# A gather-bound factorization machine: the quad that is kept raw moves from a block's eighth place to its sixth

## The chip, the core and the metric

The kernel runs on one core of one Trainium2 chip. The metric is device time in microseconds (us). The kernel before takes 735.56 us, the median of three runs (734.74 to 735.95).

## What is computed

For 2048 samples with 32 fields each, every field picks one row of 496 numbers out of its own table of 1250 rows, and the row is scaled with the sample's value of that field. Cut to what matters:

```python
gathered = table[f][xi[:, f]] for each field f      # (2048, 32, 496)
e  = gathered * xv[:, :, None]
s  = sum of e over the 32 fields
qi = 0.5 * (s * s - sum of e * e over the fields)    # (2048, 496)
h  = relu(xv @ W1 + b1)                              # (2048, 1024)
y  = concatenate([qi, h]) @ W2 + b2                  # (2048, 1)
```

All is float32. 2048 x 32 rows of 1984 bytes are 130 MB that have to be gathered from HBM.

## The kernel before

**Blocks and quads.** The batch is cut into 16 blocks of 128 samples, and the 32 fields of a block into eight quads. A quad is four fields of 128 samples: 512 rows in four groups of 128 partitions, each group fetched by one indirect DMA. So a block has eight quads (s = 0 to 7 in the code, "first" to "eighth" in the text) and 32 gathers, and the kernel has 128 quads and 512 gathers. Engines are named as in the profile: POOL (GpSimd), ACT (ScalarE), DVE (VectorE), PE (TensorE).

**Slots.** The rows land in the buffer `gathered`, which has eight slots. The quad with the running number n uses slot n % 8, so a block's quad s reuses the slot of the previous block's quad s. POOL issues the gathers in order (L218). Ahead of a quad's four gathers it waits until the slot's old quad is squared and has been summed (L210 to L214): for most quads the second is the semaphore `added`, raised by DVE, and for the quads of `block_quads` it is `summed`, raised by PE.

**Two ways through a block.** Seven of the quads are scaled in place (by ACT, L234, and the fifth by DVE, L447) and added up in PSUM by DVE (`running_ps`, L462); the last of these adds writes to `added_up` in SBUF. The one quad that is left, `block_quads = (7,)`, stays raw: ACT squares it with the value as a scale (L247), and PE sums it with the weights as the operand (L328, `sum_quad`). PE also sums `added_up` over the fields (L341, `sum_fields`), both into `sum_ps`. The last matmul of `sum_quad` raises `summed`. ACT then squares `sum_ps` (L254, `square_sums`), and that raises `sum_squared_ready`.

**Squares.** ACT squares the first quad from PSUM (L291), the second to fourth in one instruction of 5952 elements per partition (L241), and the fifth to seventh likewise. DVE weighs all squares with W2 (L435, eight instructions for a block).

**The hidden layer.** PE multiplies the block's values by W1 (L362, two instructions) and raises `hidden_ready`; DVE weighs the result with W2 (L528) and raises `hidden_used`.

**The order.** Each engine's instructions are written out in order, and every dependence between engines is a semaphore wait; there is no planner. PE's order in block i is: hidden layer of i (after `hidden_used` of i-1), wait for `sum_squared_ready` of i-1, wait for the last add of i, `sum_fields(i)`, `sum_quad(i * 8 + 7)`. ACT reaches `square_sums(i - 1)` behind the sixth quad of block i. The last block differs: its quads five to eight all stay raw.

**Entries.** In the trace each of PE's float32 matmuls stands as two weight loads (PEld) and two matmuls (PE). So the hidden layer of a block has 8 entries, `sum_fields` 16 and `sum_quad` 16, together 40.

Of the kernel before, what the change touches and what calls it, by code (L numbers as in the profile page):

```python
# [15 lines left out]
def fm_kernel(nc, index, value, value_t, emb, w1, b1, w2, b2, out):  # L16
# [23 lines left out]
    block_quads = (7,)  # L40
    wide = [0, 1, 2, 3, 4, 5, 6]

    by_vector = 4
# [4 lines left out]

    def scaled_with(n):

        return n // quads * (adds - 1) + adds_with(n % quads) - (n % quads > by_vector)
# [6 lines left out]
    def last_add(n):  # L58

        return n % quads == (3 if n // quads == end else 6)  # L60
# [3 lines left out]
    square_of = {0: 1, 1: 2, 2: 2, 3: 2, 7: 3, 4: 4, 5: 4, 6: 4}  # L64
    end_square_of = {0: 1, 1: 2, 2: 2, 3: 2, 4: 3, 5: 4, 6: 5}

    def squared_with(n):
        i, s = divmod(n, quads)
        return i * 4 + (end_square_of if i == end else square_of)[s]
# [6 lines left out]
    with ExitStack() as ctx:  # L76
# [82 lines left out]
        normed = sem("normed")  # L159
        summed = sem("summed")  # L160
# [30 lines left out]
        def _(pool):  # L191
# [9 lines left out]
            for i in range(blocks):  # L201
                if i < 2:

                    pool.wait_ge(index_ready, i + 1)
                for s in range(quads):
                    n = i * quads + s
                    if n >= slots:


                        pool.wait_ge(squared, squared_with(n - slots))  # L210
                        if by_tensor(n - slots):
                            pool.wait_ge(summed, (n - slots) // quads + 1)
                        else:
                            pool.wait_ge(added, adds_with(n - slots))  # L214
                    for j in range(GROUPS):
                        g = i * in_block + s * GROUPS + j
                        arrival = last_fetched[j // pairs] if n == all_quads - 1 else fetched[n % slots]
                        nc.gpsimd.indirect_dma_start(  # L218
                            out=gathered[:, n % slots, j, :], out_offset=None, in_=emb,
                            in_offset=bass.IndirectOffsetOnAxis(ap=index_rows[:, g:g + 1], axis=0),  # L220
                        ).then_inc(arrival, 16)

        @block.scalar
        def _(act):
# [37 lines left out]
            def square_scaled(n, count):  # L262
                act.wait_ge(scaled, scaled_with(n + count - 1))
                if n % quads == by_vector:
                    act.wait_ge(scaled_wide, n // quads + 1)
# [29 lines left out]
            for n in range(all_quads - 1):  # L295
# [4 lines left out]
                if by_tensor(n):  # L300
                    if s == (deep if i == end else quads - 1):
# [3 lines left out]
                elif s > 0 and s != by_vector:  # L305
# [3 lines left out]
                if s == 1:  # L309
# [5 lines left out]
                elif s == 7:  # L315
                    square_scaled(n - 3, 3)
# [7 lines left out]
        def _(pe):  # L324
            def sum_rows(n, j):
# [3 lines left out]
                                        gathered[:, n % slots, j], start=False,  # L329
                                        stop=(s == quads - 1), tile_position=(0, j * COLS))  # L330
# [7 lines left out]
            def sum_fields(i):  # L338

                for j in range(GROUPS):  # L340
                    last = nc.tensor.matmul(sum_ps[j * COLS:(j + 1) * COLS, 0:dim], own_sample[:],  # L341
                                            added_up[:, i % 2, j, :], start=True, stop=False,
                                            tile_position=(0, j * COLS))

# [13 lines left out]
            for i in range(blocks):  # L358
# [37 lines left out]
        def _(dve):  # L396
# [43 lines left out]
            def add_quad(n):  # L440
# [4 lines left out]
                elif s == by_vector:  # L445
# [5 lines left out]
                    dve.wait_ge(scaled_wide, i + 1)  # L451
# [24 lines left out]
            for j in range(GROUPS):  # L476
# [8 lines left out]
                values[:].rearrange("p (i s j) -> p s j i", s=quads, j=GROUPS)[:, by_vector]  # L485
# [8 lines left out]
            for j in range(GROUPS):  # L494

                spread(weights[:, :, j], values[:].rearrange("p (i s j) -> p i s j", s=quads, j=GROUPS
                                                             )[:, :, quads - 1, j], blocks, j)
# [16 lines left out]
            for n in range(all_quads - deep + 1):  # L514
# [9 lines left out]
                if s == 6 and i > 0:  # L524
                    weigh_sums(i - 1)
                if s == 7 or n == end * quads + 4:
# [72 lines left out]
```

## Time and profile before

| | us |
|---|---|
| median of three runs | 735.56 |
| the profiled execution, its own time | 734.71 |
| its span in the profile | 732.9 |
| POOL busy, 512 gathers of 0.946 us | 484.4 |
| DVE busy | 540.5 |
| ACT busy | 474.2 |
| PE busy | 123.1 |

The profile's page gives per engine the busy time, and in 40 slices of 18.3 us how busy each was, the clock granted to TensorE and the rate of the DMAs. Most slices move 202 to 204 GB/s; some move less, the lowest in the middle of the run 56. A view of waits adds up, per engine and line, the idle time ahead of instructions and what ended it: "issue" means nothing that the profile shows, "remote" an event that it can't put to an instruction. The timeline lists instructions by start. The idle time ahead of an instruction stands in brackets.

### The profile page before, as it was taken

The page shows a single profiled execution, that of the slowest core. Times are in us where ns is not written, and L with a number is a line of the kernel's source. Part 1 is how long each engine was busy: PE and PEld are TensorE (multiplying, and loading weights), DVE is VectorE, ACT ScalarE, POOL GpSimd, SP SyncE. Part 2 cuts the span into 40 slices and gives each one's busy share as a digit, 9 for nine tenths or more (in the row PEclk, how much of TensorE's full clock was granted, in tenths as well). Part 3 has the DMA queues.
Part 4 walks back from the last instruction along what each step waited for, and adds up shares of the span by engine and source line. Part 5 has one row for each costly group of instructions (what it writes and reads, how often), then busy time and mean ns, then how long its engine had stood idle before and what let it go on. Part 6 is the DMA issues. An engine that isn't in the chain of part 4 may idle for free.

```text
span 732.9 us, 2598 instructions
## 1 busy us (share of the span) xinstructions
PE 123.1 (17%) x374; PEld 29.6 (4%) x374; DVE 540.5 (74%) x463; ACT 474.2 (65%) x516; POOL 485.9 (66%) x524
## 2 busy tenths in 40 slices
PE   2030020300303003030211302203030220400315
PEld 0000000000000000000000000001000000000001
DVE  4675969595398683988969396396978849549684
ACT  0877775771875837778683863868777394567871
POOL 6777775762767737777774754777777474677760
PEclk9995555555555555555555555555555555555557
DMA  7777775772766737777774763777777474577760
GB/s 226 203 204 203 204 203 158 203 204 56 202 192 185 205 102 204 203 204 204 203 202 128 202 179 98 203 203 204 203 204 202 126 203 132 145 203 203 203 190 0
DMA packets 33683, 131.93 MB, mean 180 GB/s; under 512 B 8641, under 2 KB 8769, under 8 KB 33634
## 3 DMA queue, kind: packets, MB, share of 16 engines
q0 software_dynamic: 32768, 130.06, 64.6%
q1 hardware_dynamic: 800, 1.31, 0.6%
q10 hardware_dynamic: 98, 0.40, 0.2%
q14 instruction: 14, 0.11, 0.0%
q8 instruction: 3, 0.05, 0.0%
HBM read 131.72 MB, written 0.01 MB: 180 GB/s over the span
## 4 chain that ended last, share of the span: by engine, by line
POOL 39%; issue 23%; another core or an unknown queue 6%; PE 3%; DVE 2%; ACT 1%; DMA 0%; POOLq 0%
POOL gathered L218 39%; DVE running_ps L462 1%; PE sum_ps L328 1%; PE hidden_ps L349 1%; ACT squares L241 1%; ACT squares L247 1%; PE hidden_ps L362 1%; PE sum_ps L341 1%; DMA gathered<-emb,index_rows 0%; DVE squares L435 0%; DVE gathered L447 0%; POOLq L214 0%; DVE weighted_late L547 0%; DVE weighted L421 0%
## 5 line engine op out<-in xcount | busy, mean ns | idle before, releaser
L218 POOL DMA_INDIRECT gathered<-emb,index_rows x512 | 484.4, 946 | 224.1 <-issue 155.8
L462 DVE SCALAR_TENSOR_TENSOR running_ps<-gathered,running_ps 128x1984 f32<-128x1984 f32 x77 | 171.4, 2226 | 146.7 <-issue 107.6
L435 DVE SCALAR_TENSOR_TENSOR squares<-squares,w_ps 128x1984 f32<-128x1984 f32 (+1 forms) x128 | 276.7, 2167 | 0.0
L234 ACT ACTIVATE gathered<-gathered,values 128x496 f32<-128x496 f32 x312 | 194.5, 695 | 25.5 <-DMA gathered<-emb,index_rows 23.3
L241 ACT ACTIVATE squares<-gathered 128x5952 f32<-128x5952 f32 x31 | 159.8, 5156 | 36.8 <-DMA gathered<-emb,index_rows 34.3
L341 PE MATMUL sum_ps<-added_up,own_sample 128*32 128x496 f32 x128 | 30.1, 1031 | 550.3 <-issue 431.0
L247 ACT ACTIVATE squares<-gathered,values 128x496 f32<-128x496 f32 x76 | 47.4, 696 | 67.4 <-DMA gathered<-emb,index_rows 63.2
L362 PE MATMUL hidden_ps<-w_b,value_rows 33*128 33x512 f32 x64 | 55.3, 1011 | 42.4 <-issue 20.8
L234 ACT ACTIVATE running_ps<-gathered,values 128x496 f32<-128x496 f32 x64 | 39.5, 662 | 33.7 <-issue 18.7
L254 ACT ACTIVATE sum_squared<-sum_ps 128x496 f32<-128x496 f32 x16 | 9.2, 573 | 71.0 <-remote 58.4
L462 DVE SCALAR_TENSOR_TENSOR added_up<-gathered,running_ps 128x1984 f32<-128x1984 f32 x16 | 35.5, 2219 | 25.4 <-ACT gathered L234 25.0
L447 DVE SCALAR_TENSOR_TENSOR gathered<-gathered,running_ps 128x1984 f32<-128x1984 f32 x15 | 33.3, 2217 | 0.0
L291 ACT ACTIVATE squares<-running_ps 128x1984 f32<-128x1984 f32 x16 | 29.2, 1823 | 1.4
L328 PE MATMUL sum_ps<-gathered,weights 128*32 128x496 f32 x120 | 28.2, 1026 | 9.2 <-DMA gathered<-emb,index_rows 9.2
L341 PEld LDWEIGHTS sum_ps<-added_up,own_sample 128*32 128x32 f32 x128 | 3.6, 139 | 574.6 <-issue 574.6
L528 DVE SCALAR_TENSOR_TENSOR weighted_hidden<-hidden_ps,w_all 128x1024 f32<-128x1024 f32 x16 | 19.5, 1221 | 4.4 <-remote 4.4
L362 PEld LDWEIGHTS hidden_ps<-w_b,value_rows 33*128 33x128 f32 x64 | 16.5, 284 | 81.3 <-issue 65.8
L234 ACT ACT_TABLE_LOAD x1 | 1.3, 1283 | 17.1 <-DMA gathered<-emb,index_rows 17.1
L421 DVE SCALAR_TENSOR_TENSOR weighted<-sum_squared,w_ps 128x496 f32<-128x496 f32 x16 | 10.7, 667 | 0.0
L435 DVE DVE_READ_ACCUMULATOR squares<-squares,w_ps 128x1 f32 x128 | 10.6, 83 | 0.0
L349 PE MATMUL hidden_ps<-squares,own_sample 128*32 128x496 f32 x24 | 7.9, 789 | 2.4 <-issue 2.2
L328 PE MATMUL sum_ps<-gathered,end_weights 128*32 128x496 f32 x32 | 8.0, 813 | 0.0
(40 smaller groups left out, 27.0 us busy)
## 6 DMA issues: line engine op xcount, KB each, us to landing
gathered<-emb,index_rows POOLq DMA_INDIRECT x512
w_all<-w SPq DMA_DIRECT2D x1, 760.0 KB
values<-value SPq DMA_DIRECT2D x1, 256.0 KB, 2.9
value_rows<-value_t ACTq DMA_DIRECT2D x1, 256.0 KB
index_raw<-index SPq DMA_DIRECT2D x1, 240.0 KB, 4.3
w_b<-w ACTq DMA_DIRECT2D x1, 128.0 KB
index_raw<-index SPq DMA_DIRECT2D x1, 16.0 KB, 2.5
w_b<-b ACTq DMA_DIRECT2D x1, 4.0 KB
```

What stands on the lines that cost most here:

```text
L218: nc.gpsimd.indirect_dma_start(out=gathered[:, n % slots, j, :], out_offset=None, in_=emb, in_offset=bass.IndirectOffsetOnAxis(ap=index_ro ...
L234: return nc.scalar.mul(running_ps[:, j, 0:dim] if s == 0 else rows_of_one, rows_of_one, values[:, g:g + 1])
L241: return nc.scalar.activation(squares[:, s // deep, kept, groups], gathered[:, held, groups], ACT.Square)
L247: return nc.scalar.activation(squares[:, s // deep, s % deep, j], gathered[:, n % slots, j], ACT.Square, scale=values[:, g:g + 1])
L291: nc.scalar.activation(squares[:, 0, 0], running_ps[:, :, 0:dim], ACT.Square).then_inc(squared, 1)
L328: return nc.tensor.matmul(sum_ps[j * COLS:(j + 1) * COLS, 0:dim], operand, gathered[:, n % slots, j], start=False, stop=(s == quads - 1), ...
L341: last = nc.tensor.matmul(sum_ps[j * COLS:(j + 1) * COLS, 0:dim], own_sample[:], added_up[:, i % 2, j, :], start=True, stop=False, tile_po ...
L362: last = nc.tensor.matmul(hidden_ps[:, h, :], value_rows[:, i * P:(i + 1) * P], w1_b1[:, h * 512:(h + 1) * 512], start=True, stop=True)
L435: return nc.vector.scalar_tensor_tensor(of, of, -0.5, w2_ps[:, 0:dim].unsqueeze(1).to_broadcast([P, quads_of.stop - quads_of.start, dim]), ...
L447: nc.vector.scalar_tensor_tensor(gathered[:, n % slots], gathered[:, n % slots], 1.0, running_ps[:, :, dim + i].unsqueeze(2).to_broadcast( ...
L462: nc.vector.scalar_tensor_tensor(added_up[:, i % 2] if last_add(n) else sums, gathered[:, n % slots], 1.0, sums, ALU.mult, ALU.add).then_i ...
L528: nc.vector.scalar_tensor_tensor(weighted_hidden[:], hidden_ps[:], 0.0, w2_all[:, dim:].rearrange("p (h c) -> p h c", h=halves), ALU.max, ...
```

## The change

The raw quad is now a block's sixth (`block_quads = (5,)`), and the seventh and eighth are scaled and added. In PE's order `sum_quad` comes ahead of `sum_fields`; its last matmul raises a new semaphore, `rows_summed`, for which POOL waits before it reuses the slot. `summed` is raised by the last matmul of `sum_fields` and has ACT and DVE as its readers. ACT squares the raw quad behind the eighth's scaling, and the fifth alone and the seventh and eighth together at the next block's first quad; so the squares take five steps in a block instead of four. On DVE, two small steps change places: L528's moves from the eighth quad to the seventh, L421's from the seventh to the eighth. The last block's own quads are worked as before.

```diff
-    block_quads = (7,)
-    wide = [0, 1, 2, 3, 4, 5, 6]
+    block_quads = (5,)
+    wide = [0, 1, 2, 3, 4, 6, 7]
...
-    square_of = {0: 1, 1: 2, 2: 2, 3: 2, 7: 3, 4: 4, 5: 4, 6: 4}
+    square_of = {0: 1, 1: 2, 2: 2, 3: 2, 5: 3, 4: 4, 6: 5, 7: 5}
...
                         if by_tensor(n - slots):
-                            pool.wait_ge(summed, (n - slots) // quads + 1)
+                            pool.wait_ge(rows_summed, (n - slots) // quads + 1)
...
-                if s == 1:
+                if s == 0 and i > 0:
+                    square_scaled(n - 4, 1)
+                    square_scaled(n - 2, 2)
+                elif s == 1:
                     square_begun(n - 1)
...
                 elif s == 7:
-                    square_scaled(n - 3, 3)
+
+                    place_free(n)
+                    square_quad(n - 2)
...
-                pe.wait_ge(added, adds_with(i * quads + (3 if i == end else 6)))
-                sum_fields(i)
                 if i < end:
-                    sum_quad(i * quads + 7).then_inc(summed, 1)
+                    sum_quad(i * quads + block_quads[0]).then_inc(rows_summed, 1)
+
+                pe.wait_ge(added, adds_with(i * quads + (3 if i == end else 7)))
+                last = sum_fields(i)
+                if i < end:
+                    last.then_inc(summed, 1)
```

The first place is PE's order in one block (the third). Before, the hidden layer is followed by the field sums and then by the raw quad:

```order
L362 MATMUL hidden_ps<-w1_b1,value_rows 128x512 [waits hidden_used]
L362 MATMUL hidden_ps<-w1_b1,value_rows 128x512
L341 MATMUL sum_ps<-added_up,own_sample 32x496 [waits added,sum_squared_ready]
L341 MATMUL sum_ps<-added_up,own_sample 32x496 x3
L328 MATMUL sum_ps<-gathered,weights 32x496 [waits fetched7]
L328 MATMUL sum_ps<-gathered,weights 32x496 x3
```

Now, in the same place (L377 is the hidden layer, L342 the raw quad, L355 the field sums):

```order
L377 MATMUL hidden_ps<-w1_b1,value_rows 128x512 [waits hidden_used]
L377 MATMUL hidden_ps<-w1_b1,value_rows 128x512
L342 MATMUL sum_ps<-gathered,weights 32x496 [waits fetched5,sum_squared_ready]
L342 MATMUL sum_ps<-gathered,weights 32x496 x3
L355 MATMUL sum_ps<-added_up,own_sample 32x496 [waits added]
L355 MATMUL sum_ps<-added_up,own_sample 32x496 x3
```

The wait for ACT's square of the last block's sums stands ahead of the raw quad now, and the wait for the last add behind it. The number of matmuls is the same.

The second place is ACT's order from the fifth quad of a block on. Before:

```order
L241 ACTIVATE squares<-gathered 128x5952 [waits scaled,fetched4]
L234 ACTIVATE gathered<-gathered,values 128x496 [waits fetched5]
L234 ACTIVATE gathered<-gathered,values 128x496 x3
L254 ACTIVATE sum_squared<-sum_ps 128x496 [waits sum_squared_used,summed]
L234 ACTIVATE gathered<-gathered,values 128x496 [waits fetched6]
L234 ACTIVATE gathered<-gathered,values 128x496 x3
L247 ACTIVATE squares<-gathered,values 128x496 [waits normed,fetched7]
L247 ACTIVATE squares<-gathered,values 128x496 x3
L241 ACTIVATE squares<-gathered 128x5952 [waits scaled_wide,scaled]
```

Now (L250 squares scaled quads, L263 the sums, L243 scales, L256 squares the raw quad):

```order
L250 ACTIVATE squares<-gathered 128x5952 [waits scaled,fetched4]
L263 ACTIVATE sum_squared<-sum_ps 128x496 [waits sum_squared_used,summed,fetched5]
L243 ACTIVATE gathered<-gathered,values 128x496 [waits fetched6]
L243 ACTIVATE gathered<-gathered,values 128x496 x3
L243 ACTIVATE gathered<-gathered,values 128x496 [waits fetched7]
L243 ACTIVATE gathered<-gathered,values 128x496 x3
L256 ACTIVATE squares<-gathered,values 128x496 [waits normed]
L256 ACTIVATE squares<-gathered,values 128x496 x3
L250 ACTIVATE squares<-gathered 128x1984 [waits scaled_wide,scaled,fetched0]
L250 ACTIVATE squares<-gathered 128x3968 [waits scaled]
```

The square of the sums comes one scaling earlier after the squares of the second to fourth quads, and the last squares of the block stand behind the landing of the next block's first quad.

## Rows read from the trace of the kernel before

**Rows 1.** The page: engines' busy time, DMA by slice.

```profile
span 732.9 us, 2598 instructions
PE 123.1 (17%) x374; PEld 29.6 (4%) x374; DVE 540.5 (74%) x463; ACT 474.2 (65%) x516; POOL 485.9 (66%) x524
...
GB/s 226 203 204 203 204 203 158 203 204 56 202 192 185 205 102 204 203 204 204 203 202 128 202 179 98 203 203 204 203 204 202 126 203 132 145 203 203 203 190 0
```

**Rows 2.** Waits: engine, line, releaser, us in total, times, longest.

```profile
POOL gathered L218 <- issue: 155.8, 502, 3.1
POOL gathered L218 <- remote: 66.1, 7, 13.5
...
ACT sum_squared L254 <- remote: 58.4, 7, 12.4
```

**Rows 3.** Timeline around POOL's longest wait: start, us, engine, idle before.

```profile
131.44 1.91 PE L328 MATMUL sum_ps<-gathered,weights 128*32 128x496 f32 x8
...
162.40 0.95 POOL L218 DMA_INDIRECT gathered<-emb,index_rows  x1 [0.30 <-issue]
...
176.11 0.58 ACT L254 ACTIVATE sum_squared<-sum_ps 128x496 f32<-128x496 f32 x1 [12.44 <-remote]
...
176.86 0.94 POOL L218 DMA_INDIRECT gathered<-emb,index_rows  x1 [13.51 <-remote]
...
184.23 2.50 ACT L247 ACTIVATE squares<-gathered,values 128x496 f32<-128x496 f32 x4 [5.15 <-DMA gathered<-emb,index_rows]
```

**Rows 4.** Timeline, POOL: four more of its eight long waits.

```profile
219.69 0.95 POOL L218 DMA_INDIRECT gathered<-emb,index_rows  x1 [3.14 <-issue]
...
268.71 0.94 POOL L218 DMA_INDIRECT gathered<-emb,index_rows  x1 [9.38 <-remote]
...
395.70 0.94 POOL L218 DMA_INDIRECT gathered<-emb,index_rows  x1 [7.27 <-remote]
...
447.51 0.94 POOL L218 DMA_INDIRECT gathered<-emb,index_rows  x1 [12.11 <-remote]
```

**Rows 5.** Timeline, PE: the start of three of its bursts.

```profile
46.63 1.88 PE L341 MATMUL sum_ps<-added_up,own_sample 128*32 128x496 f32 x8 [28.53 <-issue]
...
319.08 1.88 PE L341 MATMUL sum_ps<-added_up,own_sample 128*32 128x496 f32 x8 [35.49 <-issue]
...
497.78 1.88 PE L341 MATMUL sum_ps<-added_up,own_sample 128*32 128x496 f32 x8 [35.94 <-issue]
```

**Rows 6.** Timeline, ACT and DVE: when they took up PE's signals.

```profile
122.91 0.58 ACT L254 ACTIVATE sum_squared<-sum_ps 128x496 f32<-128x496 f32 x1 [3.40 <-remote]
...
394.96 0.58 ACT L254 ACTIVATE sum_squared<-sum_ps 128x496 f32<-128x496 f32 x1 [6.11 <-remote]
...
406.17 1.23 DVE L528 SCALAR_TENSOR_TENSOR weighted_hidden<-hidden_ps,w_all 128x1024 f32<-128x1024 f32 x1 [1.12 <-remote]
...
446.77 0.58 ACT L254 ACTIVATE sum_squared<-sum_ps 128x496 f32<-128x496 f32 x1 [11.00 <-remote]
...
573.88 0.58 ACT L254 ACTIVATE sum_squared<-sum_ps 128x496 f32<-128x496 f32 x1 [6.32 <-remote]
...
585.09 1.22 DVE L528 SCALAR_TENSOR_TENSOR weighted_hidden<-hidden_ps,w_all 128x1024 f32<-128x1024 f32 x1 [1.11 <-remote]
```

**Rows 7.** Lines by form: shapes, count, busy us, mean ns, idle before.

```profile
L462 DVE SCALAR_TENSOR_TENSOR running_ps<-gathered,running_ps 128x1984 f32<-128x1984 f32 x77 | 171.4, 2226 | 146.7 <-issue 107.6 <-ACT squares L291 35.4 <-ACT gathered L234 3.0
L241 ACT ACTIVATE squares<-gathered 128x5952 f32<-128x5952 f32 x31 | 159.8, 5156 | 36.8 <-DMA gathered<-emb,index_rows 34.3 <-issue 2.4
L291 ACT ACTIVATE squares<-running_ps 128x1984 f32<-128x1984 f32 x16 | 29.2, 1823 | 1.4
```

**Rows 8.** Timeline, POOL's last gather, and where PE and ACT stand behind it.

```profile
710.21 0.94 POOL L218 DMA_INDIRECT gathered<-emb,index_rows  x1 [0.30 <-issue]
...
720.44 1.35 PE L349 MATMUL hidden_ps<-squares,own_sample 128*32 128x496 f32 x3 [2.22 <-issue]
```

More of the change, by code:

```diff
@@ L47, in by_tensor, with scaled_wide_with @@
         return n % quads in (end_quads if n // quads == end else block_quads)
+    by_scalar = [s for s in wide[1:] if s not in by_vector]
     def scaled_with(n):
-        return n // quads * (adds - 1) + adds_with(n % quads) - (n % quads > by_vector)
+        i, s = divmod(n, quads)
+        return i * len(by_scalar) + max(sum(k <= s for k in by_scalar), 1)
+    def scaled_wide_with(n):
+        i, s = divmod(n, quads)
+        return i * len(by_vector) + sum(k <= s for k in by_vector)
     def adds_with(n):
@@ L68, in squared_with @@
         i, s = divmod(n, quads)
-        return i * 4 + (end_square_of if i == end else square_of)[s]
+        return i * 5 + (end_square_of if i == end else square_of)[s]
     lines = blocks * GROUPS
@@ L159, in fm_kernel @@
         normed = sem("normed")
+        rows_summed = sem("rows_summed")
         summed = sem("summed")
@@ L263, in square_scaled @@
                 act.wait_ge(scaled, scaled_with(n + count - 1))
-                if n % quads == by_vector:
-                    act.wait_ge(scaled_wide, n // quads + 1)
+                if any(n % quads <= s < n % quads + count for s in by_vector):
+                    act.wait_ge(scaled_wide, scaled_wide_with(n + count - 1))
                 square(n, count, slice(0, GROUPS)).then_inc(squared, 1)
@@ L299, in _ @@
                 act.wait_ge(fetched[n % slots], (n // slots + 1) * 16 * GROUPS)
-                if by_tensor(n):
-                    if s == (deep if i == end else quads - 1):
+                if i == end and s >= deep:
+                    if s == deep:
                         place_free(n)
                     square_quad(n)
-                elif s > 0 and s != by_vector:
+                elif s in by_scalar:
                     if s == 1:
@@ L328, in sum_rows @@
                 return nc.tensor.matmul(sum_ps[j * COLS:(j + 1) * COLS, 0:dim], operand,
-                                        gathered[:, n % slots, j], start=False,
-                                        stop=(s == quads - 1), tile_position=(0, j * COLS))
+                                        gathered[:, n % slots, j], start=(i < end),
+                                        stop=(n == all_quads - 1), tile_position=(0, j * COLS))
             def sum_quad(n):
@@ L522, in _ @@
                     weigh_half(h, j)
-                if s == 6 and i > 0:
+                if s == 7 and i > 0:
                     weigh_sums(i - 1)
-                if s == 7 or n == end * quads + 4:
+                if s == 6 or n == end * quads + 4:
                     dve.wait_ge(hidden_ready, i + 1)
```

15 lines of the change are left out of this document (8 added, 7 removed).

## The prediction

> **What bounds the kernel now.** I read the page first [rows 1]. No engine is busy all the time: DVE 540.5 us, POOL 485.9, ACT 474.2 of a span of 732.9. The DMA rate is flat at about 203 GB/s, with dips down to 56. A flat ceiling with holes asks two questions: what sets the ceiling, and what makes the holes.
>
> The ceiling is POOL's own pace. A gather takes 0.95 us and 0.30 us lie between two [rows 3], so 1.25 us each, 5.0 us for a quad and 40 us for a block. 512 gathers are 640 us. The holes are in the view of waits [rows 2]: POOL stood 66.1 us for something "remote", 7 times. One more wait, 3.14 us, is booked as issue [rows 4]. Together 69.2 us in eight waits; less the 0.30 us that each gap has anyhow, that is 66.8 us. POOL's first gather starts at about 4 us, its last ends at 711.2 [rows 8], and 4.3 + 640 + 66.8 = 711.1. So the span is POOL's pace, plus the eight waits, plus a tail of 21.7 us. ACT's and DVE's work is hidden below that, and only the waits and the tail can change.
>
> Each of the eight waits stands ahead of a block's eighth quad, in the blocks 2, 3, 4, 5, 8, 9, 12 and 13 (counted from 0), which follows from the number of gathers ahead of them. It is the only place where POOL waits for `summed`. The longest shows it [rows 3]: POOL stops at 163.35 and goes on at 176.86, and ACT, which waits for the same semaphore at L254, starts at 176.11 after 12.44 us. Yet PE's matmuls that raise it ended at 133.35. They were not late; the signal came 42.8 us after them.
>
> **The pace of PE's signals.** This is what the change has to be measured by. Between ACT's start on `summed` at 394.96 and DVE's on `hidden_ready` at 406.17 lie 11.21 us; again 11.21 us from 573.88 to 585.09 [rows 6]. Between these two signals PE has 8 entries, so 1.40 us per entry. From the burst at 319.08 [rows 5] to the signal at 394.96 are 72 entries (32 + 8 + 32) in 75.9 us, which is 54.2 entries at that pace, so 17.8 went ahead of it for free. The burst at 46.63 and the signal at 122.91 give 17.5, 497.78 and 573.88 give 17.6. So I read PE as an engine whose finished entries are passed on in order, some 17.5 at once and then one per 1.40 us: a signal comes at S + 1.40 x (N - 17.5), S being the start of the burst where the count begins and N the entries up to it. A block has 40 entries, 56 us at this pace, against 40 us of gathers. Lateness grows by 16 us per block until something ends it.
>
> What ends it: with N = 112 the rule gives 451.4 for the signal that ACT took at 446.77, and 178.9 for that at 176.11. POOL had then stood for 11.4 and 12.8 us with no gather landing. After the wait that ends at 268.71 it was 8.6 us [rows 4]; at the end, PE stalls until 720.44 and then runs, 9.3 us after the last gather [rows 8]. POOL's stand of 6.5 us ahead of 394.96 ended nothing, since the next signal still came 11.21 us later. So a stand of some 10.8 us releases everything. The first burst after it passes for free, and the count begins anew with the next one (319.08 and 497.78).
>
> As to the Trainium skill, TensorE: Matmul & The Clock Gate ("The cost: per-tile semaphore tail") has matmuls complete in program order and an increment on the last add a tail of some tens of ns. The order agrees here, the tail doesn't: the trace has 42.8 us. By that page `summed` would not be late and the change would have nothing to win.
>
> **The change part by part.** Take T as the start of a block's first gather. A quad lands 7.4 us after its first gather starts (176.86 to 184.23 [rows 3]).
>
> *PE.* Nothing is added or removed: 16 + 16 + 8 entries, in the order raw quad, field sums, next hidden layer. The raw quad lands at T + 32.4; ACT is through with the squares of three quads (5.16 us [rows 7]) and L254 (0.58) at T + 33.2, so the raw quad's burst starts there. The eighth quad lands at T + 42.4, plus ACT's scaling 2.5 and DVE's add 2.2: field sums at T + 47.1. Who waits: POOL needs `rows_summed` at T + 65 (sixth quad of the next block), ACT needs `summed` at T + 72.6.
>
> Start with block 0, S = T + 33.2 (the 8 entries of the first hidden layer are long gone):
> - block 1: rows_summed has N = 56, comes at T + 87.1, needed at 105. On time.
> - block 1: summed, N = 72, 109.5, needed at 112.6. On time.
> - block 2: rows_summed, N = 96, 143.1, needed at 145. On time.
> - block 2: summed, N = 112, 165.5, needed by ACT at 152.6. ACT stands 12.9 us. POOL is not touched: it needs ACT's next squares at T + 180, and ACT has them at 175.4 (two scalings, raw quad, fifth).
> - block 3: rows_summed, N = 136, 199.1, needed at 185. 14.1 us late, plus 0.75 us from signal to gather (176.11 to 176.86). The release comes before, at 10.8, so 11.5 us in block 4.
>
> After it the raw burst of block 4 passes for free and the count starts at its field sums, T + 47.1 of that block. rows_summed of block 7 then has N = 120, comes at 190.6, needed at 185: 6.3 us with the 0.75, in block 8. The next, N = 160, comes at 246.6, needed at 231.3: again cut by the release to 11.5 us, in block 9. So 17.8 us in a cycle of five blocks (before: 7.27 + 12.11 in one of four [rows 4]). Blocks 8, 9, 13 and 14: 35.6. Sum 11.5 + 35.6 = 47.1 us against 66.8: the change is worth 19.7 us. The gain is that POOL asks for a signal that has 16 entries less ahead of it, and that ACT's wait for the other no longer falls together with POOL's.
>
> *ACT.* The squares of fifth to seventh (one instruction, 5.16 us) become the fifth alone (1.82, as L291's 1984 elements) and two together. By the per-element time of these rows the two take 3.5, so 0.15 us more for 15 blocks, 2 us in all. ACT is busy 65% of the span [rows 1], and this hides in its waits for landings; without that cover it would cost the 2 us. The slots of the fifth, seventh and eighth are now freed at the next block's first quad: the fifth's square is done at T + 49.2 and asked for at T + 60, the others' at T + 52.7 and at T + 70. The cover is 10.8 us.
>
> *DVE.* L528 and L421 change places; the same seven adds and scalings (2.2 us each [rows 7]) and eight weighings, 34 us in 40. The add of the eighth quad is now the last. begin_sums of the next block waits for it, done at T + 49.3, and ACT gets there at T + 52.7, behind its squares. Nothing on the path; the cover is 3.4 us, and an add that is late by more would move ACT only, not POOL.
>
> *The tail.* The last block's order is as before. The backlog in it is again one or two blocks old; I take 21.7 us, bounds 19 to 25.
>
> *The sum.* 4.3 + 640 + 47.1 + 21.7 = 713.1 of span. The profiled execution took 1.8 us more than its span (734.71 to 732.9), so 714.9, and lies 0.85 below the median: 716.
>
> Open sizes: the release after 8.6 or 12.8 us instead of 10.8 shifts three waits, -7 or +6. A release that is only partial, like that at 176.11, which was followed by waits of 3.14 and 9.38 [rows 4], adds 12 us each time, once or twice. 17.5 taken as 16.5 or 18.5 shifts the short waits by 1.4 each, 3 to 4 us. That is 700 to 735 for this case.
>
> **Rivals.**
>
> *The signal is on time (8%).* As the first reader's semaphore is now raised by the burst ten microseconds before the next, it might be passed on without the backlog. For: the lateness is not PE's work, and I have it from two signals only. Against: `hidden_ready` has a semaphore of its own and is on the same 1.40 us pace. It gives 734.71 - 66.8 + 0.85 = 669. The page named above would give the same for the new signal.
>
> *The waits move whole (8%).* If lateness hangs on the time and not on the count, `rows_summed` is as late as `summed` was: PE's burst and POOL's need both move about ten us earlier, and the distance, some 31 us, is the same. The eight waits of 66.8 us at the sixth quad: 736.
>
> *Slower: the release comes too late (17%).* At the eighth quad POOL and ACT stood together, ACT for 11.00 of POOL's 12.11 us. At the sixth, ACT still has three quads to square and DVE to add and weigh, for some 8 to 11 us after POOL has stopped. If the release needs a core that stands, it comes later. The point is 14.1 us: beyond it block 4 isn't released, its wait is 14.9 us, and block 5's would be 16 and is cut to 14.8 at best. Then 6.3 + 14.8 per cycle in blocks 9, 10, 14, 15: 14.9 + 14.8 + 42.2 = 71.9 us, 5.1 more than before, 741. Each release that fails altogether adds 16 more. Against: at the end PE was released while ACT and DVE were at work.
>
> **How the numbers follow.** The forecast's case has 60%. Another 7% are for a course in between, 680 to 700, with a wait or two less. Predicted 716. The range for eight in ten takes in the case's own 700 to 735, its neighbour at 736 and half of the slower one: 699 to 741. A measurement of this kernel can tell 0.2% (1.5 us) from no change. Faster: 60 + 7 + 8 = 75%. Same: 8%. Slower: 17%.
>
> **What the changed kernel's profile would show.** POOL's long waits at sixth quads, none at eighth; about five, first in block 4, the long ones near 11.5 us. ACT idle ahead of its square of the sums in the blocks before. 1.40 us per entry between PE's signals. Wrong, if POOL waits in every block or in none, if the first wait is in block 2, or if POOL waits at other quads for ACT's squares.

## The result and the profile after

The changed kernel takes 740.85 us (median of four runs, 740.22 to 741.42) against 735.15 of the kernel before beside it (732.53 to 735.95): ratio 1.0084, interval 1.0056 to 1.0111. Forecast were 716 us and a gain. The time lies at the upper edge of the range, and near the slower rival's 741.

The page of the changed kernel, answering to [rows 1]:

```profile
span 738.4 us, 2601 instructions
PE 127.6 (17%) x374; PEld 27.8 (4%) x374; DVE 541.8 (73%) x463; ACT 474.5 (64%) x531; POOL 487.2 (66%) x524
...
GB/s 226 201 204 203 203 204 202 203 201 204 79 171 203 68 196 203 204 202 203 202 204 203 150 202 204 36 203 203 113 201 203 204 204 203 202 204 203 161 62 1
```

The work is nearly the same; the holes in the rate have moved. Its waits, answering to [rows 2] (engine, line, releaser, us in total, times, longest):

```profile
POOL gathered L227 <- issue: 167.6, 503, 14.6
POOL gathered L227 <- remote: 46.7, 6, 15.5
...
ACT squares L250 <- remote: 40.5, 8, 6.7
...
ACT sum_squared L263 <- issue: 28.9, 2, 15.8
ACT squares L300 <- remote: 28.5, 5, 7.4
DVE weighted_hidden L545 <- remote: 26.6, 4, 14.5
```

New are the "remote" rows of L250 and L300: there ACT waits for `scaled`, a signal of ACT itself. In block 4, for example, ACT's scaling ended at 189.2 and `scaled` rose at 194.8. POOL's long waits in the timeline (start, us, engine, idle before), answering to [rows 4]; all six stand ahead of sixth quads, in the blocks 4, 5, 9, 10, 11 and 15:

```profile
204.27 0.95 POOL L227 DMA_INDIRECT gathered<-emb,index_rows  x1 [14.57 <-issue]
...
257.18 0.95 POOL L227 DMA_INDIRECT gathered<-emb,index_rows  x1 [13.08 <-remote]
...
422.53 0.95 POOL L227 DMA_INDIRECT gathered<-emb,index_rows  x1 [5.19 <-remote]
...
477.83 0.95 POOL L227 DMA_INDIRECT gathered<-emb,index_rows  x1 [15.53 <-remote]
...
526.18 0.95 POOL L227 DMA_INDIRECT gathered<-emb,index_rows  x1 [8.55 <-remote]
...
690.30 0.94 POOL L227 DMA_INDIRECT gathered<-emb,index_rows  x1 [4.09 <-remote]
```

Together 61.0, less 0.30 each 59.2 us, against 66.8 before: 7.6 less. The end, answering to [rows 8]:

```profile
704.07 0.95 POOL L227 DMA_INDIRECT gathered<-emb,index_rows  x1 [0.30 <-issue]
...
720.35 1.23 DVE L545 SCALAR_TENSOR_TENSOR weighted_hidden<-hidden_ps,w_all 128x1024 f32<-128x1024 f32 x1 [14.50 <-remote]
```

The last gather ends at 705.0 instead of 711.2, so 6.1 us of the smaller waits arrive there. But the tail, the time from the last gather's end to the end of the span, is 738.4 - 705.0 = 33.4 us instead of 21.7. DVE stands for the last block's `hidden_ready`, and four weighings of 2.2 us queue behind it. -6.1 + 11.7 = +5.6, and the spans differ by 5.5: that is the loss. TensorE's granted clock was 0.997 in this run and 0.553 in that of before, and the field sums' matmuls took 1034 and 1031 ns on average: the clock has no part in this.

### The profile page after: what moved, and what is told of

Read it like the earlier page. It is cut to its first block, busy times and chain, and to the rows that moved or that the text cites. A ratio compares the mean times of both kernels' runs of the same rounds, so it can differ in the third digit from the quotient of the medians.

```text
span 738.4 us, 2601 instructions
## 1 busy us (share of the span) xinstructions
PE 127.6 (17%) x374; PEld 27.8 (4%) x374; DVE 541.8 (73%) x463; ACT 474.5 (64%) x531; POOL 487.2 (66%) x524
## 4 chain that ended last, share of the span: by engine, by line
POOL 39%; ACT 20%; issue 18%; another core or an unknown queue 10%; DVE 8%; ACTq 2%; DMA 2%; POOLq 0%; PE 0%; DVEq 0%
POOL gathered L227 39%; ACT gathered L243 9%; ACT squares L250 6%; DVE squares L452 4%; DVE running_ps L479 3%; ACTq L262 2%; ACT running_ps L243 2%; ACT squares L256 2%; ACT squares L300 1%; DMA gathered<-emb,index_rows 1%; DVE added_up L479 1%; DVE gathered L464 1%; DMA index_raw<-index 0%; DVE weighted L438 0%
## 5 line engine op out<-in xcount | busy, mean ns | idle before, releaser
L479 DVE SCALAR_TENSOR_TENSOR running_ps<-gathered,running_ps 128x1984 f32<-128x1984 f32 x77 | 171.5, 2228 | 157.8 <-issue 103.2
L243 ACT ACTIVATE gathered<-gathered,values 128x496 f32<-128x496 f32 x312 | 193.4, 696 | 66.3 <-DMA gathered<-emb,index_rows 61.2
L250 ACT ACTIVATE squares<-gathered 128x5952 f32<-128x5952 f32 (+2 forms) x46 | 161.5, 3542 | 66.6 <-remote 40.5
L342 PE MATMUL sum_ps<-gathered,weights 128*32 128x496 f32 x120 | 28.2, 1033 | 354.4 <-issue 203.8
L355 PE MATMUL sum_ps<-added_up,own_sample 128*32 128x496 f32 x128 | 30.1, 1034 | 228.2 <-issue 182.9
L377 PE MATMUL hidden_ps<-w_b,value_rows 33*128 33x512 f32 x64 | 60.4, 1097 | 14.3 <-DVE value_rows L518 14.3
L300 ACT ACTIVATE squares<-running_ps 128x1984 f32<-128x1984 f32 x16 | 29.2, 1824 | 34.2 <-remote 28.5
L263 ACT ACTIVATE sum_squared<-sum_ps 128x496 f32<-128x496 f32 x16 | 9.2, 577 | 61.9 <-issue 28.9
L256 ACT ACTIVATE squares<-gathered,values 128x496 f32<-128x496 f32 x76 | 47.2, 695 | 1.4 <-issue 1.4
L243 ACT ACTIVATE running_ps<-gathered,values 128x496 f32<-128x496 f32 x64 | 39.4, 662 | 9.3 <-issue 9.3
L377 PEld LDWEIGHTS hidden_ps<-w_b,value_rows 33*128 33x128 f32 x64 | 18.7, 321 | 55.0 <-issue 55.0
L342 PEld LDWEIGHTS sum_ps<-gathered,weights 128*32 128x32 f32 x120 | 3.0, 140 | 378.0 <-issue 237.0
L355 PEld LDWEIGHTS sum_ps<-added_up,own_sample 128*32 128x32 f32 x128 | 3.2, 140 | 254.9 <-issue 206.4
L342 PE MATMUL sum_ps<-gathered,end_weights 128*32 128x496 f32 x32 | 5.8, 805 | 7.1 <-DVE weighted_hidden L545 7.1
```

Of the source, the lines that this page charges most:

```text
L243: return nc.scalar.mul(running_ps[:, j, 0:dim] if s == 0 else rows_of_one, rows_of_one, values[:, g:g + 1])
L250: return nc.scalar.activation(squares[:, s // deep, kept, groups], gathered[:, held, groups], ACT.Square)
L256: return nc.scalar.activation(squares[:, s // deep, s % deep, j], gathered[:, n % slots, j], ACT.Square, scale=values[:, g:g + 1])
L300: nc.scalar.activation(squares[:, 0, 0], running_ps[:, :, 0:dim], ACT.Square).then_inc(squared, 1)
L342: return nc.tensor.matmul(sum_ps[j * COLS:(j + 1) * COLS, 0:dim], operand, gathered[:, n % slots, j], start=(i < end), stop=(n == all_quad ...
L377: last = nc.tensor.matmul(hidden_ps[:, h, :], value_rows[:, i * P:(i + 1) * P], w1_b1[:, h * 512:(h + 1) * 512], start=True, stop=True)
```

## The experiments

These runs met five chips. On three of them the kernel before takes 732 to 736 us, with the late signals of the prediction ("late chips"); on two it takes 661.5 us. Which kind a run met is said each time, since it turned out to decide more than any edit.

An "entry" is one record of an instruction in the trace. An engine's "row" is my name for the entries that it has finished and whose signals have not come yet. In the diffs, "..." stands for lines left out.

### Is it PE's row of entries? (late chip, before 733.6 us)

`fields_one`: one of a block's four field-sum matmuls instead of four, PE 28 entries instead of 40.

```diff
...
-                for j in range(GROUPS):
+                for j in range(GROUPS if i == end else 1):
```

> The changed kernel, with only one of the four field-sum matmuls of each block but the last (three quarters of these sums are left out): PE has 28 entries for a block instead of 40. Theory A (PE's entries are passed on at one per 1.40 us, whatever they do): 28 x 1.40 = 39.2 us for a block of 40, no backlog grows, so POOL's waits at the sixth quad (59 us) and the late hidden-layer signal at the end (some 12 us) both go: 667 to 675 us. Theory B (a signal from PE is late by its place in time, not by the count): waits as in the changed kernel, 735 to 741 us.

744.24 us, ratio 1.0146 (1.0108 to 1.0184), where neither theory had it. PE's row is gone: `rows_summed` rises 0.04 us after its matmul. The waits at sixth quads are gone with it, and others are there:

```profile
POOL gathered L227 <- ACT squares L250: 61.2, 11, 5.8
...
ACT squares L300 <- remote: 95.7, 12, 8.4
ACT squares L250 <- remote: 71.2, 12, 6.0
```

From block 5 on POOL waits 5.8 us at each block's second quad (and 1.1 at the fifth), and blocks come every 46.2 us. ACT has 33 entries in a block (24 scalings, 4 squares of raw rows, 4 other squares, 1 of the sums), and 33 x 1.40 = 46.2. So I read ACT as having a row of its own, at the same pace, which PE's had hidden.

`narrow`: the same matmuls over 16 of 496 columns in 14 blocks; the same entries, less work.

```diff
...
+                wide_as = 16 if 0 < i < end else dim
...
-                                        gathered[:, n % slots, j], start=(i < end),
...
+                                        gathered[:, n % slots, j, 0:wide_as], start=(i < end),
...
```

> The changed kernel, with PE's raw-quad and field-sum matmuls in blocks 1 to 14 over 16 columns instead of 496 (the other columns of the sums are left out): as many entries as in the changed kernel, much less work in each. Theory A (count of entries): no change, 738 to 742 us. Theory C (PE is really busy for longer than its entries show, by the columns it streams): the waits shrink with the work, 670 to 700 us.

741.03 us, ratio 1.0103 (1.0073 to 1.0133), with PE busy for 82.9 instead of 127.6 us and the same six waits (longest 16.3). The lateness isn't PE's work. That is what the count of entries gives.

`act_few`: ACT scales a quad in one instruction instead of four, with the values of the first group for all four.

```diff
-                for j in range(GROUPS):
-                    last = scale(n, j)
-                last.then_inc(scaled, 1)
+                rows_of_all = gathered[:, n % slots]
+                g = n // quads * in_block + n % quads * GROUPS
+                nc.scalar.mul(rows_of_all, rows_of_all, values[:, g:g + 1]).then_inc(scaled, 1)
```

> The changed kernel, with each of ACT's scalings of a quad in one instruction instead of four (all four groups with the first group's values, so the numbers differ from the reference): 15 entries fewer of ACT in a block, the same data. Theory D (each engine has a queue and a pace of its own): PE's signals and POOL's waits stay, ACT's own late signals (6 us idle ahead of its squares) go, 733 to 741 us. Theory E (the engines share one path for their finished entries): PE's pace rises above one per 1.40 us and the waits shrink, under 715 us.

741.02 us, ratio 1.0102 (1.0064 to 1.014). ACT's waits for its own `scaled` are gone, as a row per engine wants it, and POOL's six waits at sixth quads stay, though in part in other blocks (longest 15.6; 69.0 us in all, less 0.30 each). Relieving one engine alone wins nothing.

`own_signal`: the kernel before, its raw quad still the eighth, but summed ahead of the field sums and with `rows_summed`.

```diff
+                if i < end:
+                    sum_quad(i * quads + 7).then_inc(rows_summed, 1)
                 pe.wait_ge(added, adds_with(i * quads + (3 if i == end else 6)))
-                sum_fields(i)
+                last = sum_fields(i)
                 if i < end:
-                    sum_quad(i * quads + 7).then_inc(summed, 1)
+                    last.then_inc(summed, 1)
```

> The kernel before, with one part of the change alone: the raw quad stays the eighth, but is summed ahead of the field sums and has its own signal, for which POOL waits. Theory A: the count up to the slot's signal is 16 lower, as in the change, but ACT's signal from the field sums comes up to 20 us late, while ACT still has to square the fifth to seventh quads behind it: waits at the fifth quads appear. 725 to 745 us. Rival (own signal and order bring the gain, the place costs it): under 725 us.

738.85 us, ratio 1.0061 (1.0025 to 1.0098). Its ten times fall into two groups, five at 733.7 to 736.5 us and five at 741.2 to 743.9, and both granted clocks, about 0.55 and 0.99, occur in each. The signal of its own alone doesn't help in either group. In the profile, one of the upper group, POOL's waits sum to 68.6 us, with 33.7 "remote" and 28.8 for ACT's squares at fifth quads among them.

### Two chips without late signals

Of `both_few` (the edits of `fields_one` and `act_few` together), `act_more` and `no_end_wait` the first runs fell on a chip where before takes 661.61 us. All three took 661.3 to 662.1, and POOL had no wait over 0.3 us. They said nothing of entries, and were repeated below. Of the first of them this was expected:

> The changed kernel with one field-sum matmul a block instead of four (PE 28 entries a block, 39.2 us at 1.40) and each of ACT's scalings of a quad as one instruction (15 entries fewer a block, about 19, 27 us). Left out: three of four groups' field sums and the right values of three of four groups. Theory Q (each engine passes on its own finished entries, one per 1.40 us, beyond some 17.5): both are under the 40 us of a block's gathers, POOL has no long wait anywhere, and the span is 4.3 + 640 + a tail of 20 to 33: 665 to 678 us. Rival R (the two changes were each answered by a limit that is not in the count, something common to the core that keeps every kernel at some 740): 735 to 745 again, with waits of POOL at yet another quad.

Neither theory was right in its reason: the kernel before took the same there. `two_vector` ran there too: no raw quad, all eight are scaled and added, two of them by DVE.

```diff
-    block_quads = (5,)
...
+    block_quads = ()
...
-    by_vector = (4,)
+    by_vector = (4, 6)
...
-                        running_ps[:, :, dim + i].unsqueeze(2).to_broadcast([P, GROUPS, dim]),
+                        (running_ps[:, :, dim + i] if s == by_vector[0] else
+                         values[:, n * GROUPS:(n + 1) * GROUPS]).unsqueeze(2).to_broadcast([P, GROUPS, dim]),
```

> Computes the whole reference. From the changed kernel: no raw quad (all eight are scaled and added), the fifth and the seventh scaled by DVE, the squares of a block's fifth to eighth in one instruction at the next block's first quad. Entries a block: PE 24 (33.6 us at 1.40), ACT 28 (39.2), DVE 20 to 22 (28 to 31), all under 40; DVE's work rises to some 38.4 of 40 us. Theory Q: no backlog, no long wait of POOL, 4.3 + 640 + 22 to 33 of tail, and up to 30 us for DVE's fuller row: 668 to 700. Rival R (a limit that follows no count): 735 to 745. If DVE is over 40 us a block, POOL waits for `added`, and the time is 16 times DVE's period.

686.31 us, ratio 1.038 (1.0365 to 1.0394): it met a cost of its own. Its gathers took 991 ns instead of 946 (lines of `two_vector`):

```profile
L222 POOL DMA_INDIRECT gathered<-emb,index_rows x512 | 507.5, 991 | 157.5 <-issue 153.5 <-ACT squares L295 2.1 <-DVE index_rows L418 1.8
...
L452 DVE SCALAR_TENSOR_TENSOR gathered<-gathered,values 128x1984 f32<-128x1984 f32 x15 | 33.3, 2220 | 0.0
```

The second row is the one instruction of the loop that reads two operands from SBUF. Each of the 15 ran into one gather, which took 2.2 to 2.8 us, as here:

```profile
90.68 2.22 DVE L452 SCALAR_TENSOR_TENSOR gathered<-gathered,values 128x1984 f32<-128x1984 f32 x1
91.06 2.65 POOL L222 DMA_INDIRECT gathered<-emb,index_rows  x1 [0.30 <-issue]
```

In `two_psum`, described below, its values lie in PSUM. There, and in `dve_tail` on a chip of the same kind as this one, the gathers are back at 946 ns (in `two_psum` up to the fifth block; what comes behind has another cause, below). The Trainium skill, SBUF — State Buffer ("Reading the diagram:"), has a DVE instruction with two SBUF inputs hold, for its whole length, a port pair that it shares with GpSimd, against GpSimd work that reads SBUF. The trace agrees: the gathers read their row numbers from `index_rows` in SBUF, and were longer by 23 us in all.

The changed kernel and the kernel before, both as they are, on the second chip of this kind:

> The changed kernel, as it is. With late signals: 740 to 744, 0.8 to 1.2% over the kernel before. Without: within 0.2% of it, 661 to 662.

> The kernel before, as it is. With late signals: POOL's eight long waits at the same eighth quads, in the blocks 2, 3, 4, 5, 8, 9, 12 and 13, within 1.5 us each, whatever the granted clock is. Without (661): no wait of POOL over 0.3 us, last gather at 644, tail 17.

661.29 us, ratio 0.9996 (0.9986 to 1.0006). Its waits, and those of before (profile of `before_again`, span 660.0 at a granted clock of 0.622; the changed kernel 659.8 at 0.999), the changed kernel first:

```profile
POOL gathered L227 <- issue: 155.3, 510, 0.3
```

```profile
POOL gathered L218 <- issue: 148.3, 487, 0.3
```

Both end their last gather at 644.2 to 644.3 us. There `rows_summed` and `summed` of the changed kernel rise within 0.06 us of their last matmul's end. So ACT's split squares and the exchanged adds cost nothing there, and the whole loss hangs on the late signals. Whether these belong to the chip or to the time at which it was used is not separated: kernels that ran on a chip one after the other agreed, one late chip was late again 24 minutes later, and the other four were each used once.

The changed kernel on one more late chip:

> The changed kernel once more, as it is. Where the kernel before runs at 732 to 735 us: 740 to 741 again. Where it runs at 661 to 662: if the change's cost is in the late signals alone, POOL never waits for more than 0.3 us, the tail is the same, and the two agree within 0.2%: 661 to 662. If the change costs something of its own (ACT's split squares, the exchanged adds), it is 1 us or more above.

743.84 us against 735.88, ratio 1.0113 (1.0094 to 1.0132), last gather's end at 709.6, tail 32.7: the same picture, 3 us slower than expected.

### POOL has a row too

`two_psum` is `two_vector` with the seventh quad's values in PSUM. It computes the whole reference, with PE at 24 entries a block and ACT at 28 (20 + 4 scalings, 3 squares, 1 of the sums), both under 40 us.

```diff
...
+                    if s == by_vector[1] and i % 4 == 0:
+                        step(nc.vector.tensor_copy(
+                            w2_ps[:, dim:dim + 4 * GROUPS].rearrange("p (i j) -> p i j", j=GROUPS),
+                            values[:].rearrange("p (i s j) -> p i s j", s=quads, j=GROUPS)[:, i:i + 4, s]))
...
```

> Computes the whole reference. As the kernel with eight added quads and two of them scaled by DVE (686.3 us, POOL's gathers 991 ns instead of 946), but the values of the second of these quads lie in PSUM too, copied there once in four blocks, so that no DVE instruction of the loop reads two operands from SBUF. If it was that instruction (15 of 2.22 us) that made the gathers longer, by (509.0 - 485.8) / 15 = 1.5 us each, the gathers are back at 946 ns and the time without late signals is 661 to 664. If the longer gathers come from DVE's fuller row, it stays at 680 to 687. With late signals (before at 732 to 735): PE 24 entries a block, ACT 28, both under 40 us at 1.40, so 661 to 680 by the count; 735 to 745 if the loss follows no count.

733.37 us against 735.88, ratio 0.997 (0.9959 to 0.9982); on another late chip (`two_psum_b`) 731.54 against 732.8, ratio 0.9967 (0.9951 to 0.9982). That is neither the 661 to 680 of the count nor the 735 to 745 of the rival. The timeline of its gathers in the fourth and in the eighth block:

```profile
119.80 0.95 POOL L222 DMA_INDIRECT gathered<-emb,index_rows  x1 [0.30 <-issue]
121.05 0.94 POOL L222 DMA_INDIRECT gathered<-emb,index_rows  x1 [0.30 <-issue]
...
299.39 1.08 POOL L222 DMA_INDIRECT gathered<-emb,index_rows  x1 [0.30 <-issue]
300.77 1.10 POOL L222 DMA_INDIRECT gathered<-emb,index_rows  x1 [0.30 <-issue]
302.17 1.09 POOL L222 DMA_INDIRECT gathered<-emb,index_rows  x1 [0.30 <-issue]
```

POOL waits nowhere for more than 0.9 us, but a gather takes longer. From the 193rd to the last start they come every 1.402 us on average. With 17.5 ahead for free at 1.25 us each, the limit should bite at the 163rd; the first longer one is the 164th (the 175th to 180th in three later profiles). By the rule the last gather comes at 4.6 + 494.5 x 1.40 = 696.9 us; it ended at 697.2 (694.8 to 695.5 in the three).

`both_few_b` takes the same test with DVE's work as in the changed kernel (540 us, in `two_psum` 603):

> The kernel with one field-sum matmul a block and one instruction for each of ACT's scalings once more (PE 28, ACT 19 entries a block; left out: three of four groups' sums and values). What the last job added: with PE at 24 and ACT at 28 entries POOL did not wait, but from its 160th gather on its own gathers came every 1.40 instead of 1.25 us, as if its own row were passed on at the same pace. Theory Q with POOL's own row: the last gather ends at 4.3 + 512 x 1.40 - 17.5 x 1.40 = 696.6, the tail is 20 to 34 us, so 719 to 733 us. Theory Q without POOL's row (the slower gathers of that kernel came from DVE's fuller row, 603 us of work against 540 here): 665 to 678. Where the kernel before runs at 661: 661 to 662.

731.53 us, ratio 0.9976 (0.9961 to 0.9992), the last gather's end at 695.5. POOL's row it is, and not DVE's.

`act_more_b`: `fields_one` and four more ACT instructions of one column per block, 37 entries.

```diff
+                    for j in range(GROUPS):
+                        nc.scalar.mul(spare[:, j:j + 1], values[:, j:j + 1], values[:, j:j + 1])
```

> The kernel with one field-sum matmul a block (744 us, blocks every 46.2 us) and four one-column ACT instructions more in 15 blocks once more. Theory Q: blocks every 51.8 us as soon as ACT's row is late, so 800 to 830 us. Rival W (ACT's signals are late for its work): 744 to 750. Where the kernel before runs at 661: 662.

742.24 us (739.61 and 744.87), ratio 1.0115 (1.0055 to 1.0175): the 800 to 830 us did not come. The late signals moved (POOL waits at second and fifth quads of the blocks 3 to 5, 8, 9, 12 and 13, 7.4 us at most), but the blocks did not come every 51.8 us. Single ones did: between the second quads of the blocks 4 and 5 and of 12 and 13 lie 51.8 us, and 52.5 between those of 8 and 9. After each the period fell to 46 and then to 40. The pattern repeats after four blocks and 179.4 us, which is 44.9 a block. So the pace fits where a row holds, but an entry more has no fixed price: something releases the rows.

### The tail

`no_end_wait_b`: DVE doesn't wait for the last block's hidden layer.

```diff
+                    if i == end:
+                        nc.vector.memset(hidden_part[:, i:i + 1], 0.0).then_inc(hidden_used, 1)
+                        continue
                     dve.wait_ge(hidden_ready, i + 1)
```

> The changed kernel without DVE's wait for the last block's hidden layer once more (its part of the last 128 samples is left out, PE's matmuls stay). If that signal alone makes the tail 33 instead of 21.7 us: 11 us less than the changed kernel, 729 to 733. If PE's row holds the end anyhow (112 entries of the last rows' sums follow): 738 to 744. Where the kernel before runs at 661: 662.

734.27 us, ratio 1.0014 (0.9998 to 1.0029). Its last gather ends at 707.2 and its span at 732.7, a tail of 25.6 us. So this wait, with the one instruction behind it (1.2 us) that is left out too, holds 7 to 8 of the 11.7 us (33.4 and 32.7 on the other late chips); the other 4 stay open. It isn't the only way to a long tail: in `fields_one` DVE doesn't stand there, and the tail is 32.3 us.

`dve_tail` is `two_psum` with the last block's late squares weighed by DVE, so that PE has 80 entries instead of 128 at the end.

```diff
...
-                late_squares(n)
...
+            for j in range(GROUPS):
+                step(weigh_squares(end, 1, j, slice(0, deep - 1), late_norm[:, j:j + 1]))
```

> Computes the whole reference. The kernel with eight added quads (731.5 and 733.4 us; POOL paced at 1.40 us from the 160th gather on, last gather's end at 695.5 to 697.2, tail 34.3), and DVE weighs the squares of the last block's fifth to seventh quads itself in the tail, where it stood for 24.7 us; so PE has 48 entries less after the last field sums, 80 instead of 128. Theory Q: PE's last 16 entries that ran one per 1.40 us (from 700.8 to 723.1 in the trace of that kernel) are gone, the tail is 17 to 26 us, 714 to 724. Rival: the tail is held by something that ends late whatever PE has to do (ACT's last squares, a stand that has to pass), 731 to 734. Where the kernel before runs at 661: 658 to 664.

It met a chip without late signals and took 673.36 us against 661.44, ratio 1.0173 (1.0156 to 1.019), where 658 to 664 was expected: its tail is 27.0 us, since DVE's weighings, four of 1.7 us more, come last. So it is a version for late chips alone. On a late chip:

> Computes the whole reference; eight added quads, and DVE weighs the squares of the last block's fifth to seventh quads (PE 80 instead of 128 entries after the last block's sums begin). Without late signals its tail was 27.0 us, of which 7 are DVE's own four weighings. With late signals, Theory Q: last gather's end at 695.5 to 697.2 and the tail hardly longer than those 27: 723 to 729 us, against 731.5 to 733.4 for the kernel with all 128 entries. Rival (the tail's length with late signals isn't PE's row): 34 of tail and the 7 of DVE more, 735 to 742. Where the kernel before runs at 661: 673 again.

727.5 us against 734.38, ratio 0.9916 (0.9891 to 0.9941): the fastest there, below both kernels. Its tail is 725.4 - 694.8 = 30.6 us, `two_psum`'s was 34.3. PE's weight loads at the end, of `two_psum`:

```profile
704.93 0.11 PEld L333 LDWEIGHTS sum_ps<-gathered,end_weights 128*32 128x32 f32 x1 [2.00 <-issue]
...
707.73 0.13 PEld L333 LDWEIGHTS sum_ps<-gathered,end_weights 128*32 128x32 f32 x1 [2.69 <-issue]
...
710.53 0.13 PEld L333 LDWEIGHTS sum_ps<-gathered,end_weights 128*32 128x32 f32 x1 [2.67 <-issue]
```

With a matmul between each two, PE itself runs one entry per 1.40 us. In `dve_tail_b` PE isn't held: its last 32 matmuls on the rows run from 694.0 to 698.9. The late signals remain:

```profile
713.75 0.17 DVE L551 TENSOR_TENSOR norm_lines<-late_norm,norms 128x4 f32<-128x4 f32 x1 [6.70 <-remote]
...
720.95 0.58 ACT L257 ACTIVATE sum_squared<-sum_ps 128x496 f32<-128x496 f32 x1 [22.20 <-remote]
```

The first waits for a signal of DVE's own (`normed`), so DVE's signals are late as well; the second for PE's `summed`, 22 us after its matmul.

## Why the prediction was wrong

**The pace and the count held.** `rows_summed` rose at 91.2, 147.2 and 203.2 us, 56.0 apart, where S + 1.40 x (N - 17.5) gives 91.0, 147.0 and 203.0. The first wait came in block 4, where it was forecast. Only sixth quads are hit.

**The release failed.** This is the step "a stand of some 10.8 us releases everything". In block 4 POOL stood for 14.57 us and `rows_summed` came by the count, 13.5 us after POOL had stopped; in block 10 POOL stood for 15.53, and the signal came at 477.1 us, where the count gives 477.8. In the blocks 5 and 11 a release did come, after 12.3 and 7.8 us: `rows_summed`, `summed` and `hidden_ready` rose together, at 256.4 to 256.6 and at 525.4 to 525.6 us, where the count gives 259.2 and 533.1 for the first of them. So no length of POOL's stand tells the one from the other. The six waits are 59.2 us instead of 47.1. The prediction's reading of the two stands before, "with no gather landing", wasn't right either: rows landed for the first 2.5 us or so of each.

The slower rival had the waits of block 4 and 5 nearly right, 14.9 and 14.8 us against 14.57 and 13.08, but its ground, that a release needs a core that stands, is not borne out. While POOL stands in block 4, ACT and DVE stand first and then go on:

```profile
194.87 1.82 ACT L300 ACTIVATE squares<-running_ps 128x1984 f32<-128x1984 f32 x1 [5.68 <-remote]
...
201.81 2.23 DVE L479 SCALAR_TENSOR_TENSOR running_ps<-gathered,running_ps 128x1984 f32<-128x1984 f32 x1 [0.72 <-ACT gathered L243]
```

But both were at work too when the releases of block 5 and block 11 came:

```profile
253.67 5.16 ACT L250 ACTIVATE squares<-gathered 128x5952 f32<-128x5952 f32 x1 [1.78 <-remote]
255.68 2.23 DVE L479 SCALAR_TENSOR_TENSOR running_ps<-gathered,running_ps 128x1984 f32<-128x1984 f32 x1
...
520.87 4.89 ACT L243 ACTIVATE gathered<-gathered,values 128x496 f32<-128x496 f32 x8
523.14 2.21 DVE L452 SCALAR_TENSOR_TENSOR squares<-squares,w_ps 128x1984 f32<-128x1984 f32 x1
```

What releases the rows stays open. The rival's 741 us was luck: its waits were 12.7 us too high, and the tail, which it left as it was, 11.7 too low.

**The tail was taken over.** "I take 21.7 us, bounds 19 to 25" was 33.4, outside them. The sum of the four terms was 4.3 + 640 + 47.1 + 21.7; measured are 4.3 + 641.5 + 59.2 + 33.4. The two mis-sized terms are 12.1 and 11.7 us, 23.8 of the 25.3 that the span was off. I had the rule at hand and didn't run it to the last `hidden_ready`. From `rows_summed` of block 14, at 689.5 us, the 24 entries up to it give 723.1; DVE took it up at 720.35.

**Most of the gain was not there to be had.** "The ceiling is POOL's own pace", 1.25 us a gather, is true on a chip without late signals. On the others POOL has a row of its own, for which the sum had no term. The four profiles in which it never waited for a late signal (`two_psum` twice, `both_few_b`, `dve_tail_b`) end their last gather at 694.8 to 697.2 us, 14 to 16 ahead of the 711.2 of before. So taking away all eight waits, 66.8 us, won only some 15; the rest came back as longer gathers. The rival with the signal on time, whose last gather ends at 644, fails on that. My forecast needs it at 691.4, which is below these four too, but they don't rule it out: it still had waits of 47.1 us, and in the kernels with such waits the gathers kept their 945 to 949 ns.

**ACT's part.** I counted PE's entries alone. ACT's 33 had no term. `fields_one` showed that they bound the kernel at 744 us as soon as PE's are cut.

**The increment's tail.** The Trainium skill, TensorE: Matmul & The Clock Gate ("The cost: per-tile semaphore tail"), cited in the prediction, gives an increment a tail of tens of ns. The trace agrees on the chip without late signals: in `after_third` the semaphores rise 13 to 54 ns after the matmul's end. On the late chips the backlog comes on top, 42.8 us in [rows 3].

**Why some chips have the signals late** was not tested. The Trainium skill, NOTIFIC — the notification-queue block ("7.1 Overflow: three behaviours, one of which stalls the engine"), describes a path for records of instructions that holds its producer back when a buffer inside fills. No run here shows that it is this one. Every execution of this case has its span from such records, so whether the signals are late without them isn't shown either.

## What to carry to other kernels

Before a wait is priced as a gain, ask what the waiting engine would do with the time: run the same limit on that engine itself, and on each engine that takes over when the first is relieved. A backlog is followed up to the last signal of the program, since the tail inherits it. A release that was read from two waits is not yet a rule. And a kernel whose signals come tens of us behind their instructions is compared on more than one chip before a change is judged: here the same pair gave 1.0084, 1.0113 and 0.9996.

## What the runs showed that I had not expected

- The same kernel takes 732 to 736 us on three chips and 661 to 662 on two, while its instructions last the same (the changed kernel's DVE adds 2228 and 2227 ns, ACT's scalings 696 and 695).
- On the slower three, the entries of PE, ACT and POOL are passed on at one per 1.40 us beyond some 17.5 while a backlog lasts: PE 56.0 us for 40, ACT 46.2 for 33, POOL 1.402 per gather. Something ends a backlog early at times.
- Eleven kernels with 24 to 40 PE entries and 18 to 37 ACT entries a block all took 727 to 744 us there (medians).
- DVE instructions with both inputs in SBUF, 15 of 2.2 us each, lengthened POOL's gathers by 23 us in all; with one input in PSUM the loss was gone.
